# Second attention: ScalarE normalises the tokens by scale and bias per row, GpSimd forms root and shift

## What is computed

```python
x = L0_output                                        # (16, 256, 128)
h = _layernorm(x, axis=-1) * (1 + ca) + sa           # (x - m) / sqrt(v + eps), per token
qkv = h @ qkv_w.T + qkv_b                            # 16 heads of 8
for i, o in enumerate(OFFSETS):                      # 0..32, 48, 64, 96, 128, 192
    qk = einsum('bhnd,bhnd->bhn', q, _shift(k, o))
    lg = qk * inv * (1.0 + qs[..., i]) + pos_bias[i]
p = softmax(logits)
out = sum(p[..., i] * _shift(v, o_i)) * if_gain
gate = sigmoid(h @ gate_w.T + gate_b)
x = x + ga * ((out * gate) @ out_w.T + out_b)
```

## Time and profile before

| | us |
|---|---|
| median of 3 runs | 1267.58 |
| the runs | 1264.09, 1267.73, 1267.58 |
| the profiled execution, whole time | 1262.74 |
| its span, first to last instruction | 1261.0 |
| second attention in it, about | 760 to 1097 |
| busy over the span: PE, DVE, ACT, POOL | 1019.7, 798.9, 550.6, 566.9 |
| mean granted clock of TensorE | 0.886 |

### The profile page before, as it was taken

The page is one execution under the profiler, slowest core; times in us unless marked ns, Lnnn a source line. Parts: engine busy times, 40 slices in busy tenths (PEclk is TensorE's granted clock), DMA queues, the critical chain, the costliest instruction groups (busy, mean ns, idle before and its releaser), DMA issues. The chain is left out here.

```text
span 1261.0 us, 24378 instructions
## 1 busy us (share of the span) xinstructions
PE 1019.7 (81%) x9153; PEld 605.1 (48%) x9153; DVE 798.9 (63%) x1845; ACT 550.6 (44%) x1023; POOL 566.9 (45%) x652
## 2 busy tenths in 40 slices
PE   3777789999999999999999994898988999554330
PEld 2333344444444444444444442787777888443220
DVE  4445566766765767657555652898898889456122
ACT  1124455555455545455555433556655654211110
POOL 4535646466545664553534344533233230016446
PEclk9978799999999999999999995689899989755565
DMA  4685554446253544432613122423223221041332
GB/s 125 183 177 103 106 127 108 102 111 144 62 143 93 121 100 95 116 97 70 186 45 101 61 83 63 159 87 104 70 86 103 70 85 53 13 123 40 92 98 78
DMA packets 90052, 125.52 MB, mean 100 GB/s; under 512 B 10634, under 2 KB 58688, under 8 KB 86224
## 3 DMA queue, kind: packets, MB, share of 16 engines
q1 hardware_dynamic: 69072, 86.50, 27.2%
q10 hardware_dynamic: 18816, 34.09, 9.3%
q0 software_dynamic: 2048, 3.37, 0.9%
HBM read 92.10 MB, written 32.25 MB: 99 GB/s over the span
## 5 line engine op out<-in xcount | busy, mean ns | idle before, releaser
L542 POOL TENSOR_TENSOR a_gw<-a_half,a_wb 128x512 f32<-128x512 f32 x128 | 163.5, 1277 | 260.9 <-ACT a_half L629 204.6
L584 ACT ACTIVATE a_pr<-ps 128x512 f32<-128x512 f32 x192 | 114.4, 597 | 133.7 <-PE ps L713 131.7
L1002 DVE TENSOR_REDUCE a_nmax<-ps 128x2 f32<-128x512 f32 (+1 forms) x192 | 130.9, 685 | 57.4 <-PE ps L724 57.3
L1149 DVE SCALAR_TENSOR_TENSOR a_up<-a_th,ps 128x512 f32<-128x512 f32 x136 | 93.0, 684 | 95.0 <-PE ps L861 92.0
L848 PE MATMUL ps<-a_e_hT,e_wg 128*128 128x512 f32 x272 | 147.8, 625 | 0.3 <-ACT a_th L631 0.3
L861 PE MATMUL ps<-a_e_hT,e_wu 128*128 128x512 f32 x272 | 144.2, 612 | 1.2 <-DVE a_wT L1131 1.2
L870 PE MATMUL ps<-a_hm,e_wd 128*128 128x512 f32 x272 | 143.5, 609 | 0.7 <-DVE a_hm L1155 0.7
L629 ACT ACTIVATE a_half<-ps 128x512 f32<-128x512 f32 x136 | 80.9, 595 | 108.0 <-PE ps L848 104.3
L1701 POOL TENSOR_TENSOR a_prod<-a_q,a_kp 128x768 f32<-128x768 f32 (+1 forms) x32 | 55.6, 1758 | 112.3 <-PE ps L1909 108.9
L1155 DVE TENSOR_TENSOR a_hm<-a_up,a_gw 128x512 f32<-128x512 f32 x128 | 94.8, 741 | 14.3 <-POOL a_gw L542 10.1
L680 PE MATMUL ps<-a_mask,identb 128*128 128x256 bf16 (+1 forms) x192 | 65.1, 339 | 35.9 <-DVE a_nmax L1002 16.8
(11 more groups left out here) (266 smaller groups left out, 2061.7 us busy)
## 6 DMA issues: line engine op xcount, KB each, us to landing
a_wb<-e_wT_d ACTq DMA_DIRECT2D x128, 256.0 KB, 3.2
a_gw<-a_gd_d SPq DMA_DIRECT2D x16, 1024.0 KB, 4.9
a_qs<-a_terms_d SPq DMA_DIRECT2D x32, 384.0 KB, 5.6
a_ks<-a_terms_d SPq DMA_DIRECT2D x32, 384.0 KB, 6.6
a_gd_d<-a_gc SPq DMA_DIRECT2D x64, 132.0 KB, 2.5
a_terms_d<-a_parts SPq DMA_DIRECT2D x32, 192.0 KB, 2.2
a_terms_d<-a_parts SPq DMA_DIRECT2D x32, 128.0 KB, 2.2
a_terms_d<-a_parts SPq DMA_DIRECT2D x32, 64.0 KB, 1.9
```

Source lines behind the costliest of these rows:

```text
L542: nc.gpsimd.tensor_tensor(gw[:, par], half[:, par], wb[:, (u - 1) % RING], ALU.mult).then_inc(weighted, 1)
L584: nc.scalar.activation(dst, src, ACT.Exp).then_inc(exp_done, 1)
L1002: nc.vector.tensor_reduce(dst, src, AX_X, ALU.max, negate=True).then_inc(m_read, 1)
L1149: nc.vector.scalar_tensor_tensor(up[:, par], th[:, par], 1.0, ps[:, U_BANK], ALU.add, ALU.mult).then_inc(up_done, 1)
```

## The change

`normalise` of the second attention moves from VectorE to ScalarE, which computes rstd * x + shift in one activation for each tile of 128 tokens, with a scale and a bias per token. The shift is -mean * rstd; GpSimd forms it with two more instructions behind the power, a product and a subtraction from a tile of zeros. In ScalarE's order `normalise` stands between `projected` and `exps`. VectorE keeps `statistics` and `moments`; `statistics` gets a wait for the `moments` of the batch before and a small write to a tile `pause`, `moments` a wait for GpSimd's fourth step of the batch before, and GpSimd's `rstd_of` one for ScalarE's `normalise` of the batch before. GpSimd also waits once for the setup before its first body.

```diff
--- before.py
+++ after.py
@@ -1606,6 +1606,8 @@
         th, gs = sb("th", [P, L]), sb("gs", [P, L])
         og, yo = sb("og", [P, L]), sb("yo", [P, L])
         gd = s["a1_gd"]
+        shift, pause = sb("shift", [P, TB]), sb("pause", [P, 1])
+        none = sb("none", [P, TB])
 
         setup, cleared = sem("setup"), sem("cleared")
         stats_done, rstd_done, y_done = sem("stats_done"), sem("rstd_done"), sem("y_done")
@@ -1668,6 +1670,7 @@
             nc.gpsimd.memset(kx[:, :, :, 0:QB], 0.0)
             nc.gpsimd.memset(kp[:, :, 0:PAD], 0.0)
             nc.gpsimd.memset(hT[:, :, 0:PAD], 0.0)
+            nc.gpsimd.memset(none[:], 0.0)
             nc.gpsimd.memset(one[:], 1.0).then_inc(setup, 1)
             nc.gpsimd.memset(vb[:], 0.0).then_inc(cleared, 1)
             pool.wait_ge(cleared, 1)
@@ -1688,9 +1691,14 @@
 
             def rstd_of(b):
                 pool.wait_ge(stats_done, b.x + 1)
+                hold(pool, y_done, 1, b, 0)
                 nc.gpsimd.tensor_tensor(rstd[:], mv[:, :, 1], s["eps"][:, 0:TB], ALU.add).then_inc(rstd_done, 1)
-                pool.wait_ge(rstd_done, b.x * 2 + 1)
+                pool.wait_ge(rstd_done, b.x * 4 + 1)
                 nc.gpsimd.tensor_tensor(rstd[:], rstd[:], s["pm5"][:, 0:TB], ALU.pow).then_inc(rstd_done, 1)
+                pool.wait_ge(rstd_done, b.x * 4 + 2)
+                nc.gpsimd.tensor_tensor(shift[:], mv[:, :, 0], rstd[:], ALU.mult).then_inc(rstd_done, 1)
+                pool.wait_ge(rstd_done, b.x * 4 + 3)
+                nc.gpsimd.tensor_tensor(shift[:], none[:], shift[:], ALU.subtract).then_inc(rstd_done, 1)
 
             def products(b):
 
@@ -1704,6 +1712,7 @@
                                                         ap=[list(a.ap[0]), [step, n], [1, L]]), ALU.mult)
                 m.then_inc(prod_done, 1)
 
+            pool.wait_ge(setup, 1)
             run(pool, [("S", products), ("L", rstd_of)])
 
         @block.scalar
@@ -1714,6 +1723,14 @@
                 act.wait_ge(a_full, b.x * 2 + 1)
                 nc.scalar.activation(hT[:, b.k % 4, PAD:], ps[:, 4, 0:L], ACT.Identity, bias=sa[:], scale=ca[:]
                                      ).then_inc(hT_done, 1)
+
+            def normalise(b):
+                act.wait_ge(rstd_done, b.x * 4 + 4)
+                for k in range(TB):
+                    at = bass.ds(b.x * TB + k, 1)
+                    a = nc.scalar.activation(y[:, k, :], x[:, at, :].rearrange("p a d -> p (a d)"), ACT.Identity,
+                                             bias=shift[:, k:k + 1], scale=rstd[:, k:k + 1])
+                a.then_inc(y_done, 1)
 
             def queries_keys(b):
 
@@ -1771,7 +1788,7 @@
                 a.then_inc(v_done, 1)
 
             run(act, [("T", take_p(0)), ("T", take_p(1)), ("A", modulate), ("T", take_p(2)), ("T", take_p(3)),
-                      ("A", queries_keys), ("A", factors), ("T", gate), ("D", projected), ("X", exps),
+                      ("A", queries_keys), ("A", factors), ("T", gate), ("D", projected), ("L", normalise), ("X", exps),
                       ("X", values)])
 
         @block.tensor
@@ -1952,6 +1969,8 @@
             nc.vector.tensor_scalar(kb[:], aw["kmask"][:], bcol[:, 1:2], None, ALU.mult).then_inc(setup, 1)
 
             def statistics(b):
+                hold(v, stats_done, 1, b, 0)
+                nc.vector.memset(pause[:], 0.0)
                 for k in range(TB):
                     nc.vector.bn_stats(stat[:, k, :], x[:, bass.ds(b.x * TB + k, 1), :].rearrange("p a d -> p (a d)")
                                        ).then_inc(dve_a, 1)
@@ -1959,18 +1978,12 @@
             def moments(b):
                 v.wait_ge(dve_a, b.x * TB + TB)
                 hold(v, hT_done, 1, b, 0)
+                hold(v, rstd_done, 4, b, 0)
                 nc.vector.tensor_copy(ca[:], modT[:, 1, 1, bass.ds(b.x, 1)])
                 nc.vector.tensor_copy(sa[:], modT[:, 1, 0, bass.ds(b.x, 1)])
                 for k in range(TB):
                     n = nc.vector.bn_aggr(mv[:, k, :], stat[:, k, :])
                 n.then_inc(stats_done, 1)
-
-            def normalise(b):
-                v.wait_ge(rstd_done, b.x * 2 + 2)
-                for k in range(TB):
-                    n = nc.vector.tensor_scalar(y[:, k, :], x[:, bass.ds(b.x * TB + k, 1), :].rearrange("p a d -> p (a d)"),
-                                                mv[:, k, 0:1], rstd[:, k:k + 1], ALU.subtract, ALU.mult)
-                n.then_inc(y_done, 1)
 
             def near_logits(b):
 
@@ -2059,7 +2072,7 @@
                                         ).then_inc(x_done, 1)
 
             run(v, [("X", add_bias), ("D", gated), ("L", statistics), ("X", maxima), ("L", moments), ("X", shift),
-                    ("L", normalise), ("T", divide), ("T", weighted), ("D", residual), ("S", near_logits),
+                    ("T", divide), ("T", weighted), ("D", residual), ("S", near_logits),
                     ("S", far_logits)])
```

## The result

| | before | after |
|---|---|---|
| median of 20 runs, us | 1267.49 | 1274.56 |
| profiled execution, whole time | 1262.74 | 1272.96 |
| its span | 1261.0 | 1271.1 |
| busy: PE, DVE, ACT, POOL | 1019.7, 798.9, 550.6, 566.9 | 1016.4, 789.1, 563.7, 568.1 |

The changed kernel is slower: the ratio of the times is 1.0071 with a 95% interval of 1.0047 to 1.0095, which is +6.0 to +12.0 us. The forecast had been +7.4.

A forecast was written before the change was run, and what follows sets the result against it. Bound: one loop over TensorE and VectorE, both nearly full. 2.6 us for the eleven bodies plus 4.8 for the filling made 7.4, so a median of 1267.58 + 7.4 = 1275.0 us; range 1266 to 1280.

The forecast's parts named there:

- The sum: Whole kernel: 2.6 us in the eleven bodies and 4.8 in the filling, together 7.4 us slower, median 1275.0.
- (a): VectorE, eleven bodies: 16.1 us of normalising and root waits go, worth 0 because L2025 still waits for TensorE's outputs.
- (b): Pause write on VectorE after gated, held semaphores and extra zeros: 0 in the bodies, 0.1 us for the starting memset.
- (c): GpSimd's extra multiply and subtract: 0.55 us, with a microsecond of slack before ScalarE asks; cost 0 in the eleven bodies.
- (d): ScalarE's two activations ahead of exps: exps 0.78 us later, near_logits delayed 4.24 in all, 2.6 left for the eleven bodies.
- give-back: VectorE's add_bias, starting later, overlaps GpSimd's products less and returns 1.67 us of the 4.24 over the eleven bodies.
- a sign of being wrong: Among the listed signs that would show the forecast wrong: TensorE's pauses move; no size given.
- (e): Pipeline filling: 0.9 us before the first turn_tokens, 1.7 in the second batch, 2.2 at the first exponentials; together 4.8.
- VectorE's pace: Rival: VectorE bounds the bodies, each gives 1.46 us, 16.1 less the 4.8, time 1256.3; chance 10%.
- The late root: Rival: GpSimd's steps are held up, so ScalarE waits for the shift; about 11 us more, 1286; chance 8%.
- Covered: Rival: delays fall where TensorE pauses anyway; +0 to +3.8 us, time about 1269.5; chance 19%.

The follow-up runs named there:

- the first split: Changed kernel with ScalarE's normalise behind exps and the first two batches normalised by VectorE as before; ratio to the kernel before 0.9987 (0.9960 to 1.0015).
- the second split: Changed kernel, ScalarE's normalise still ahead of exps, with the first five batches normalised by VectorE as before; ratio to the kernel before 1.0041 (1.0013 to 1.0069).
- the longer chain: Changed kernel with two more subtractions of 128x2 on GpSimd (0.54 us) ahead of ScalarE's release; ratio to the kernel before 1.0079 (1.0054 to 1.0103).
- the logits first: Kernel before with near_logits ahead of residual on VectorE and exps ahead of projected on ScalarE; ratio to the kernel before 1.0072 (1.0047 to 1.0098).

## Why the prediction was right, point by point

**The sum.** +7.4 forecast; +9.0 by the ratio (6.0 to 12.0), +7.1 by the medians, +7.50 by the stage of the two traces. The likeliest time, 1275.0, stands against a median of 1274.56. That it fits so closely is luck. In the traces the bodies cost 1.0 where 2.6 was forecast, the filling 5.66 for 4.8, and the last bodies, put at nothing, 0.80; the errors cancel. The way and the places of the loss were right.

**(a) VectorE's freed time is worth 0.** Right as far as can be measured: it is not worth 16 us, and by the intervals at most 4 to 5, shown by taking the normalising out altogether (0.9997) and again by the first split (0.9987). The wait that takes its place is the one named, 1.65 us a body where I had said about 1.4.

**(b) Pause write and held semaphores.** Right for the bodies: with the pair behind the exponentials and VectorE normalising the first two batches, all of them still there, the ratio is 0.9987.

**(c) GpSimd's slack.** Right; 1.5 us rather than 1.0 (the pair starts one step of 0.47 behind the start of `projected`, which I had not counted), and 0.54 more are not felt.

**(d) The pair ahead of the exponentials.** B was to grow by 4.24 and grew by 4.33; nine bodies stand at 3.54 to 3.59 against the forecast 3.56. The seven bodies forecast to lengthen did so by 4.20 together. The other four, put at 0, changed by -0.28, -0.46, +0.48 and +0.39, and nearly cancel: TensorE's queue pauses inside `scores` had moved, which the prediction names as a sign of being wrong. The give-back in `add_bias` was to be 1.67; its eleven durations, 31.50 us before, sum to 29.71 after: 1.79. Here too the sum hides a miss. The seven bodies gave 1.01, and 0.73 came from the fourth, where none was forecast. The prediction had that `products` doesn't move. But it starts behind `scores`, and moved with its pauses: in the third body from 4.88 to 5.33 after `project_out`, so that nothing of 0.48 was given back, in the fourth from 6.10 to 4.95. That C shrank by 3.85 has a second source, which I had priced at nothing and which is chance too: before, `gated` waited for `gather` in two bodies in which TensorE ran at the lower clock there (C of 8.33 and 8.51 us against 7.2), after in none. So the bodies cost 1.0 us in this pair of traces and not 2.6, while the second split, with two such bodies (8.28 and 8.51), has them at 5.0 in its trace and 5.2 in its ratio. The mechanism is shown: `near_logits` moves with the pair. Its size over many executions is known only to a few microseconds.

**(e) The filling.** 4.8 forecast, 5.66 measured at the first `gated`. Its parts can be read from the first starts of TensorE's `turn_tokens` and of `near_logits`, against the stage's start: +0.92 (0.9 forecast) at the first `turn_tokens`, +3.0 at the second, +2.6 (2.6) at the first `near_logits`, +4.71 (4.7) at the second. The rest, 0.9 and not 0.1, came in the next body. The rows of after:

```profile
815.75 1.97 PE L1809 MATMUL ps<-ident,a_ex 128*128 128x128 f32 x8 [1.74 <-DVE a_lg L1994]
817.51 0.63 PE L1822 MATMUL ps<-ident,a_y 128*128 128x128 f32 x2
817.94 1.91 PE L1809 MATMUL ps<-ident,a_ex 128*128 128x128 f32 x8
819.65 1.50 PE L1828 MATMUL ps<-a_hT,a_w 128*128 128x256 f32 x4
```

and of before:

```profile
809.39 0.64 PE L1805 MATMUL ps<-ident,a_y 128*128 128x128 f32 x2
809.82 1.22 PE L1792 MATMUL ps<-ident,a_ex 128*128 128x128 f32 x8
810.87 1.03 PE L1811 MATMUL ps<-a_hT,a_w 128*128 128x256 f32 x4
```

At the same place in the program, from the second `turn_p` to the end of `project`, the granted clock was 0.91 before and 0.59 after: TensorE came to its full clock later, and the two steps took 0.69 + 0.47 = 1.2 us more. Just before them it had waited 1.74 us for the late `near_logits`, where before it had not waited; that this made the clock late is likely, but no run shows it. I had moved durations of the earlier trace rows along unchanged, and one of them was not unchanged.

**The rivals.** VectorE's pace (10%) is excluded by the kernel without normalising. The late root (8%) is excluded by the longer chain. Covered (19%) is excluded by the ratio's lower end, +6.0 us.

## What to carry to other kernels

Before work is moved off the busiest engine, read what that engine waits for next: if the next wait ends 0.1 us behind the work, the work is free where it stands. On the engine that receives it, the place in the order decides: the same 0.87 us cost the steady bodies nothing measurable behind the exponentials, and ahead of them 1.6 to 8.7 us by the second split. A step that is hidden in the steady bodies can be bare while the pipeline fills; here the five filling bodies carried 5.7 of 7.5 us in the traces (by the ratios less: 3.8 of 9.0, the rest being the 5.2 of the second split). And take a forecast sum apart before you trust that it came true.

## What the runs showed of the hardware

TensorE, though busy for 91% of the eleven bodies, was not at the full clock all the time: in seven of them it dropped to the lower level for a short while. In the part of a body where TensorE sets the pace such a drop cost 1.4 us (9.6 against 8.2), in the other between nothing and 1.8 (C of 6.71 at a granted clock of 0.75, and of 8.51 at 0.60, where `gated` waited for `gather`). From kernel to kernel the drops lay in other bodies, and with the pair twice, where five of them fell into A, they moved the total by as much as the change itself: A was 6.7 us longer.

Two instructions with inputs in on-chip memory, `products` on GpSimd and `add_bias` on VectorE, stood in each other's way where they overlapped: `add_bias` took 2.46 us alone and up to 3.53 beside `products`, which in that body (of the kernel with the logits first) took 5.26 and beside `maxima` 3.05. Keeping `products` out of `add_bias` took 4 to 5 us off part C and nothing measurable off the time.
